# A one-core attention and FFN kernel: six of its eight norms transposed by DMA

## The reference

```
x = x + tanh(g_xattn[0]) * attention(layernorm(x), ctx, ctx, Wq, Wk, Wv, Wd)
x = x + tanh(g_ffn[0])   * (layernorm(x) @ dequantize(qweight).T + bias)

attention(q, k, v):            # x, ctx: 32 x 64 x 512;  32 heads in 8 groups, head size 128
    Q = (q @ Wq.T) as (b, s, 8, 4, 128);  K, V = (k @ Wk.T), (v @ Wv.T) as (b, s, 8, 128)
    scores = Q . K * 128**-0.5, causal;  probs = softmax(scores)
    return (probs . V as (b, s, 4096)) @ Wd.T
```

## Time and profile before

| | |
|---|---|
| median of 3 runs | 1074.34 us (1073.34 to 1075.73) |
| the profiled execution | 1073.39 us, its span 1071.6 us |
| TensorE busy | 1027.7 us, 96% |
| VectorE, ScalarE, GpSimd busy | 670.9, 474.8, 236.8 us |
| TensorE's granted clock | 0.994 of full speed |

### The profile page before, as it was taken

How to read it: one execution, slowest core, us unless ns; L and a number is a source line. 1 busy time by engine, 2 the same in 40 slices (tenths; PEclk the granted TensorE clock), 3 DMA queues, 4 the chain that set the end, 5 groups by cost and what they waited for, 6 DMA issues and landing times.

```text
span 1071.6 us, 20150 instructions
## 1 busy us (share of the span) xinstructions
PE 1027.7 (96%) x8000; PEld 577.8 (54%) x8000; DVE 670.9 (63%) x1361; ACT 474.8 (44%) x937; POOL 236.8 (22%) x245
## 2 busy tenths in 40 slices
PE   5899999999999999999999999999999999999995
PEld 3455554555555555555555555555555555555542
DVE  6856666666578566655566566555557655555688
ACT  5767676576534243353334323254433423333322
POOL 1545465465504100010003110010000300000013
PEclk9999999999999999999999999999999999999997
DMA  7757644435245133233321443312323332223211
GB/s 274 238 163 250 217 175 160 158 129 177 98 150 197 50 129 118 104 114 118 119 84 55 177 158 119 118 53 86 119 106 112 119 118 89 65 106 131 72 35 59
DMA packets 64251, 137.08 MB, mean 128 GB/s; under 512 B 5409, under 2 KB 38177, under 8 KB 53537
## 3 DMA queue, kind: packets, MB, share of 16 engines
q1 hardware_dynamic: 64160, 135.81, 36.9%
HBM read 93.85 MB, written 25.17 MB: 111 GB/s over the span
## 4 chain that ended last, share of the span: by engine, by line
PE 84%; DVE 7%; ACT 6%; issue 2%; DMA 0%; SPq 0%; POOL 0%; DVEq 0%; ACTq 0%; POOLq 0%
PE pa L1210 39%; PE py L1210 30%; PE av L1321 5%; PE pp L1304 2%; PE ps L1290 2%; PE py L1382 2%; PE pp L1290 2%; PE av L1358 1%; ACT junk L567 1%; ACT q L628 1%; ACT junk L577 1%; DVE q L833 1%; ACT wd L623 1%; DVE sc L879 1%; DVE sc L890 1%
## 5 line engine op out<-in xcount | busy, mean ns | idle before, releaser
L1210 PE MATMUL pa<-xT,wq 128*128 128x512 f16 x1536 | 342.4, 379 | 6.4 <-DVE q L833 3.5
L1210 PE MATMUL py<-wd,att 128*128 128x512 f16 x1488 | 337.1, 379 | 0.0
L1210 PEld LDWEIGHTS pa<-xT,wq 128*128 128x128 f16 x1536 | 146.0, 98 | 186.6 <-issue 18.9
L1210 PEld LDWEIGHTS py<-wd,att 128*128 128x128 f16 x1488 | 143.8, 98 | 156.2
L628 ACT ACTIVATE q<-pa 128x512 f16<-128x512 f32 x128 | 75.8, 592 | 249.4 <-PE pa L1210 249.4
L912 DVE SCALAR_TENSOR_TENSOR xacc<-py,f_y,xacc 128x512 f32<-128x512 f32 x128 | 95.9, 749 | 137.0 <-PE py L1210 136.9
L674 ACT ACTIVATE att<-av 128x256 f16<-128x256 f32 x256 | 80.8, 385 | 152.2 <-PE av L1321 151.8
L903 DVE SCALAR_TENSOR_TENSOR att<-av,att 128x256 f16<-128x256 f32 x256 | 93.4, 417 | 66.0 <-ACT att L674 66.0
L833 DVE SCALAR_TENSOR_TENSOR q<-pa,q 128x512 f16<-128x512 f32 x128 | 87.8, 686 | 66.6 <-ACT q L628 63.8
L1210 PE MATMUL pa<-wv,cT 128*128 128x128 f16 x1536 | 96.2, 219 | 0.0
L1210 PEld LDWEIGHTS pa<-wv,cT 128*128 128x128 f16 x1536 | 89.8, 98 | 0.9
(11 more groups left out here) (127 smaller groups left out, 1095.2 us busy)
## 6 DMA issues: line engine op xcount, KB each, us to landing
wq<-kept_q SPq DMA_DIRECT2D x24, 1024.0 KB, 7.0
wd<-kept_d SPq DMA_DIRECT2D x23, 1024.0 KB, 4.8
v_dup<-v_nat SPq DMA_DIRECT2D x128, 128.0 KB, 2.4
raw_d<-in_wdT SPq DMA_DIRECT2D x8, 1024.0 KB, 8.8
kept_q<-wq SPq DMA_DIRECT2D x8, 1024.0 KB, 7.4
kept_d<-wd SPq DMA_DIRECT2D x8, 1024.0 KB, 4.9
raw_q<-in_wqT SPq DMA_DIRECT2D x7, 1024.0 KB, 5.7
wk<-kept_k SPq DMA_DIRECT2D x24, 256.0 KB, 7.2
```

What stands on the lines that cost most here:

```text
L1210: last = pe.matmul(out, stationary(a, i), moving(b, i), start=(i == 0 and (a, b) == PASSES[0]), stop=(i == count - 1 and (a, b) == PASSES[ ...
```

## The change

The four-tile transposes of all norms but the first and the last leave TensorE and ScalarE. SyncE instead issues for each of those norms 32 DMAs with `transpose=True`, each from 128x128 of `xh` to 128x128 of `xT` (`transpose_norm`, behind `duplicate_v`). The readers of `xT` wait for their count on a new semaphore `xT_ld` (`transposed`). Norms of kind 2 now write `xh` with its columns in the order that the transposes of before picked them in (`permuted`). Block 1's norm moves from step 6 to step 5 with all its engines' work, and the FFN of blocks 0 and 1, with its stores, from g = 1 to g = 2.

```diff
@@ norm_step
-            return 6 if tb == 0 else 4
+            return 5 if tb == 0 else 4
@@ readers of xT
+        def transposed(eng, call):
+            if call == 0:
+                eng.wait_ge(xT_ok, TILES)
+            else:
+                eng.wait_ge(xT_ld, 16 * 2 * KC * TILES * call)
@@ ffn_of
-            if g == 1 and 0 < tb < BLOCKS - 1:
+            if g == 2 and 0 < tb < BLOCKS - 1:
@@ sync
+            def transpose_norm(call):
+                which, tb = NORMS[call]
+                if which == 1:
+                    wait(sp, q_mm, 4 * GROUPS * (tb - 1))
+                    wait(sp, f_mm, TILES * (tb - 1))
+                else:
+                    sp.wait_ge(q_mm, 4 * GROUPS * (tb + 1))
+                for t in range(TILES):
+                    sp.wait_ge(x_hi, TILES * call + t + 1)
+                    wait_x_lo(sp, TILES * call + t)
+                    for c in (HI, LO):
+                        for i in range(KC):
+                            sp.dma_start(xT[:, tb % 2, c, i, t * P:(t + 1) * P], xh[:, t, c, i * P:(i + 1) * P],
+                                         transpose=True).then_inc(xT_ld, 16)
...
                 if m < STEPS:
                     duplicate_v(m)
+                if norm_of(n) is not None:
+                    transpose_norm(norm_of(n))
@@ gpsimd and vector ln_lo, scalar ln_hi (output and inputs)
+            def permuted(part, t):
+                if NORMS[t // TILES][0] == 1:
+                    return part
+                return part.rearrange("p (j i) -> p i j", j=KC)
...
-                pool.tensor_tensor(xh[:, t % TILES, LO, :], xn[:, t % TILES, :], xh[:, t % TILES, HI, :],
-                                   ALU.subtract).then_inc(x_lo, 1)
+                pool.tensor_tensor(permuted(xh[:, t % TILES, LO, :], t), straight(xn[:, t % TILES, :], t),
+                                   permuted(xh[:, t % TILES, HI, :], t), ALU.subtract).then_inc(x_lo, 1)
@@ scalar
                     for t in range(TILES):
                         ln_hi(TILES * call + t, g == 0)
-                    for t in range(TILES):
-                        ln_out(TILES * call + t)
@@ tensor
-                        pe.wait_ge(xT_ok, TILES * (NORMS.index((1, tb)) + 1))
+                        transposed(pe, NORMS.index((1, tb)))
...
-                if j < 2 and n > 0 and norm_of(n - 1) is not None:
-                    pe.wait_ge(xT_ok, TILES * (norm_of(n - 1) + 1))
...
                 y_unit(n, 2)
-                if call is not None:
-                    ln_transpose(TILES * call, 4 * n + 4)
-                    ln_transpose(TILES * call + 1, 4 * n + 4)
                 y_unit(n, 3)
-                if call is not None:
-                    ln_transpose(TILES * call + 2, 4 * n + 4)
-                    ln_transpose(TILES * call + 3, 4 * n + 4)
```

More of the change, by code:

```diff
@@ L176, in build @@
         xT_mm, xT_ok = sem("xT_mm"), sem("xT_ok")
+        xT_ld = sem("xT_ld")
         q_mm, q_hi, q_lo = sem("q_mm"), sem("q_hi"), sem("q_lo")
@@ L255, in build @@
         LATE = tuple(range((BLOCKS - 2) * TILES, (BLOCKS - 1) * TILES))
+        FINAL = len(NORMS) - 1
+        def transposed(eng, call):
[3 more added lines that the diff above has]
+                eng.wait_ge(xT_ld, 16 * 2 * KC * TILES * call)
         def ffn_of(n):
             g, tb = n % GROUPS, n // GROUPS
-            if g == 1 and 0 < tb < BLOCKS - 1:
+            if g == 2 and 0 < tb < BLOCKS - 1:
                 return tb - 1
@@ L470, in split_wv, with straight @@
                 weight_lo(wv[:, g % 2, LO, :, :], raw_v[:, g % 2, :, :], wv[:, g % 2, HI, :, :], w_mul[:, g, 2:3], wv_lo)
+            def permuted(part, t):
+                if NORMS[t // TILES][0] == 1:
+                    return part
+                return part.rearrange("p (j i) -> p i j", j=KC)
+            def straight(part, t):
+                if NORMS[t // TILES][0] == 1:
+                    return part
+                return part.rearrange("p (i j) -> p i j", j=KC)
             def ln_lo(t):
                 pool.wait_ge(x_hi, t + 1)
-                pool.tensor_tensor(xh[:, t % TILES, LO, :], xn[:, t % TILES, :], xh[:, t % TILES, HI, :],
-                                   ALU.subtract).then_inc(x_lo, 1)
+                pool.tensor_tensor(permuted(xh[:, t % TILES, LO, :], t), straight(xn[:, t % TILES, :], t),
+                                   permuted(xh[:, t % TILES, HI, :], t), ALU.subtract).then_inc(x_lo, 1)
             def ln_rstd(call):
@@ L641, in v_part, with permuted, straight @@
                                scale=K_SCALE).then_inc(v_hi, 1)
+            def permuted(part, t):
+                if NORMS[t // TILES][0] == 1:
+                    return part
+                return part.rearrange("p (j i) -> p i j", j=KC)
+            def straight(part, t):
+                if NORMS[t // TILES][0] == 1:
+                    return part
+                return part.rearrange("p (i j) -> p i j", j=KC)
             def ln_hi(t, summed):
+                call = t // TILES
                 act.wait_ge(xn_ok, t + 1)
-                wait(act, xT_mm, t - TILES + 1)
-                at = NORMS[t // TILES][1] * TILES + t % TILES
-                act.activation(xh[:, t % TILES, HI, :], xn[:, t % TILES, :], ACT.Copy,
+                if call > 0 and t % TILES == 0:
+                    transposed(act, call - 1)
+                at = NORMS[call][1] * TILES + t % TILES
+                act.activation(permuted(xh[:, t % TILES, HI, :], t), straight(xn[:, t % TILES, :], t), ACT.Copy,
                                accum_out=x_sum[:, at:at + 1] if summed else None).then_inc(x_hi, 1)
             def ln_out(t):
-                act.wait_ge(xT_mm, t + 1)
+                done = t % TILES + (TILES if t >= TILES else 0)
+                act.wait_ge(xT_mm, done + 1)
                 par = NORMS[t // TILES][1] % 2
@@ L995, in ln_lo @@
                 dve.wait_ge(xn_ok, t + 1)
-                dve.tensor_tensor(xh[:, t % TILES, LO, :], xn[:, t % TILES, :], xh[:, t % TILES, HI, :],
-                                  ALU.subtract).then_inc(xd_lo, 1)
+                dve.tensor_tensor(permuted(xh[:, t % TILES, LO, :], t), straight(xn[:, t % TILES, :], t),
+                                  permuted(xh[:, t % TILES, HI, :], t), ALU.subtract).then_inc(xd_lo, 1)
             def ffn_weight(j):
@@ L1346, in ln_transpose @@
                 wait_x_lo(pe, t)
-                wait(pe, xT_ok, t - 1)
+                if t % TILES >= 2:
+                    pe.wait_ge(xT_ok, t % TILES - 1 + (TILES if t >= TILES else 0))
                 wait(pe, av_hi, av_before)
@@ L1352, in ln_transpose @@
                     for i in range(KC):
[L1353 to L1356, removed]
+                        part = xh[:, t % TILES, c, i * P:(i + 1) * P]
                         at = (c * KC + i) * P
@@ L1364, in ffn_unit @@
                 if t % TILES == 0 and t not in FFN_DVE:
-                    pe.wait_ge(xT_ok, TILES * (NORMS.index((2, t // TILES)) + 1))
+                    transposed(pe, NORMS.index((2, t // TILES)))
                 if t in FFN_DVE:
-                    pe.wait_ge(xT_ok, TILES * NORMS.index((2, t // TILES)) + t % TILES + 1)
+                    pe.wait_ge(xT_ok, TILES + t % TILES + 1)
                 if t == LATE[0]:
```

## The result

The changed kernel takes 1237.31 us in the median of four runs (1235.25 to 1242.85), beside 1075.03 us for the kernel before: a ratio of 1.152, with a 95% interval of 1.150 to 1.155. I had forecast 1138.4 us with a range up to 1200. The sign was right, the size was not. The profiled execution spans 1235.9 us, 164.3 us more than before.

What follows compares the result with a forecast made beforehand. The prediction took TensorE as the bound, busy 1027.7 of 1071.6 us. Added to the profiled 1073.39 us, 54.8 us for five norms and 9.3 for block 1 gave 1137.5; 0.95 for the median made 1138.4 us, range 1058 to 1200.

Steps and rivals of the forecast that it cites:

- What the change can give: Six norms' transposes off TensorE save 2.92 us each in two and 2.74 in four: 16.8 us at most.
- The room: SyncE's queue has 16.7 us for a norm's 32 DMAs before the next step's `wd` load makes TensorE wait.
- The price of a transposing DMA: Each holds SyncE's queue 0.95 us, the root of 0.38 x 2.4; 32 take 30.4 us a norm.
- the same formula: With c per DMA: 5 x (wait - 2.74) + 1.6, wait = 32c - 16.7; from c = 0.71, 32c - 22.7 more for block 1.
- (d): Rival: two transposing DMAs in flight on SyncE's queue, c = 1.2 us each, 1186 us; chance 0.26.
- The estimate of 1207 us: The same sum with the Trainium skill's 1309 ns for each DMA on SyncE's queue gives 1207 us.
- Rival (c): The forecast's own case: SyncE's queue time per DMA from 0.62 to about 1.1 us, 1078 to 1163 us; chance 0.37.
- GpSimd's lateness in step 6: Block 1's norm in step 5 delays GpSimd's `wd`, so step 6's first `y_unit` waits 4.5 us.
- The `wq` of step 8: Behind block 1's 32 DMAs and `kept_q`, `wq` lands at 281.8, making step 8's query product 7.7 us late.
- The permuted write: Writing `xh` with permuted columns in norms of kind 2 was allowed 0 to 2 us, in the last norm only.
- The FFN's move: Moving the FFN and its stores from step 1 to step 2 of a pass was costed at nothing.

Runs made afterwards that it cites:

- e11_block1_tensor: `e10_ffn_step1` with block 1's norm of step 6 transposed by TensorE again: 1063.32 us, 0.9903 of the kernel before.
- e4_strided_read: The changed kernel with the permuted `xh` written in address order and `xn` read in strides of four instead: 1224.09 us.
- e10_ffn_step1: The changed kernel with one transposing DMA a tile, address-order write with strided read, block 1's norm in step 6, FFN back at g = 1: 1066.44 us.
- e7_clock_whole_wait: The changed kernel with 98 overwritten filler products on TensorE before step 9's first `y_unit`, 121 in steps 13, 17, 21, 25: 1234.09 us.

## Why the prediction was wrong, point by point

- **What the change can give, 16.8 us.** It can't be read alone in any run. `e11_block1_tensor` keeps five of the six norms off TensorE, a saving of 13.9 us by my figures, and is 11.2 us faster, with a last norm that its strided read makes slower. The size holds roughly.
- **The room, 16.7 us.** Right at 32, 16 and 4 DMAs a norm. The queue's time less the wait is 21.5, 16.4, 15.2, 16.4 and 15.2 us in the five norms, 16.9 in the mean. In step 9, the first, there was more because TensorE itself came late, from the wait for queries. The place of the waits was right too.
- **The price of a transposing DMA, 0.95 us. This step failed.** It is 41.81 / 32 = 1.31 us. I took the middle between a plain issue and `v_dup`'s landing time on a scale of ratios, a choice no row backed. A price error of 0.36 us stands 32 times in each of six norms: with 1.31 in the same formula the sum is 5 x (25.2 - 2.74) + 1.6 + 19.2 = 133 us, 1207 us in all. Of the 99 us between forecast and result this is 69 by the formula, and 62 by the waits themselves (`wd` and `wq` 138.1 us, forecast 76.2). My reason for going above `v_dup`'s 0.61 (a finer cut on one side) has nothing for it either: a DMA of eight such blocks costs the same. Of the rivals, (d) with 1.2 us (1186 us) came nearest; its picture of two in flight is not shown by anything here. The estimate of 1207 us that stands under it was nearer still, and my range ended at 1200, below that. Rival (c) was also added up a little low: c = 1.1 gives 1167 us, not 1163.
- **The pages.** The Trainium skill, "VectorE: DVE Perf Modes", section "The three transpose paths", has 1309 ns for a 128x128 by DMA. The trace agrees (1.31 us each), and adds that it is a time in which the issuing queue is held. "Advanced Engine Details and Errata", section "X-Bar Transpose (TRN2)", says they are as fast as regular DMAs; here the queue needs 1.31 us where a plain one took 0.33 to 0.38, while the time to landing, 2.3 us, is about that of `v_dup`, 2.4.
- **Block 1.** GpSimd's lateness in step 6: predicted 4.5 us, 4.9 waited. The `wq` of step 8: with 1.31 us the formula gives 19.2 us, 15.1 waited. The landing it gives, 293.3, is near the 292.87 of the trace by luck: `wq` could be issued 4.2 us after `kept_q`, not 7.4, but then took 8.1, not 7.0, and the first DMA went out 1.7 us later than I had it. TensorE came 3.6 us later than in the sum, mostly because step 6's first `y_unit` ran at the lower clock (5.14 us in place of 2.75).
- **The permuted write, 0 to 2 us.** Undersized: 13.2 us by `e4_strided_read`. I looked for it only where no queue covers it, did not ask for its size (a factor of four), and overlooked that SyncE's first DMA waits for the first tile's slow halves, so that the queue starts later too. The Trainium skill, "SBUF — State Buffer", has a note on lines of 16 bytes (section "Door 1: The DMA port swizzle (why `[64,N]` ≈ `[32,N]`)") by which each access that crosses to a new line pays a penalty. The write agrees (2.5 to 2.9 us against 0.63 for 128x512); the strided read of float32 also steps 16 bytes each time, and there the penalty is far smaller (1.17 us at most in `e10_ffn_step1`).
- **The clock.** Missing from the sum: some 10 us, by the stretches of `e7_clock_whole_wait`. Before, TensorE hardly stopped and was granted 0.994 of full speed; a forecast of long waits should carry a term for what follows them.
- **The FFN's move, nothing.** 3.3 us in `e10_ffn_step1`, in a kernel without the long waits. In the changed kernel it was not measured.

By these estimates together 133 + 13 + 10 = 156 of 162 us. They are no exact sum, since the formula's 133 is 7 more than what the trace shows in its place (123.0 + 15.1 + 4.9 of waits less the 16.8 saved: 126.2).

The two traces can be compared term by term. TensorE waits 123.0 + 15.1 + 4.9 = 143.0 us for `wd`, `wq` and GpSimd, 8.5 us more for queries and 5.6 us more for high halves in the last norm; its two large groups are 19.5 us longer and its transposes 13.0 us shorter. That makes 163.6 of the 164.3 us between the two spans.

## What to carry to other kernels

Count instructions on a queue, not bytes: before moving work to DMAs, multiply the hold of one by the number in a row, and compare with the time from there to the reader of the next load in that queue. A price that no row shows and that is multiplied by 192 decides the forecast, so its upper end should be taken as seriously as its middle. And an edit that seems only to rearrange addresses, such as a permuted write, should be priced with the engine that does it.

## What the runs showed of the hardware

- A transposing DMA within SBUF holds SyncE's queue for 1.23 to 1.27 us in the median at 128x128, 128x256 and 128x1024 alike; it lands after 2.3 us and, at 128x1024, 3.1 us.
- ScalarE's 128x512 write of halves 256 bytes apart takes 2.5 to 2.9 us against 0.63 in order, and the read of its sum behind it 0.51 against 0.20 us. With the strides on the read side it takes 1.15 us.
- VectorE's work on other SBUF tiles slows while GpSimd works: such an operation then takes up to about as long as one of GpSimd's. In the changed kernel GpSimd needs 10.32 / 4 = 2.58 us for a half, and VectorE's 0.43 us become 2.58; with GpSimd's in-order writes before, 5.05 / 4 = 1.26 us and 1.27 (the last two rows of this section). So it is not the strided write alone that does this; the write makes it last longer. The operations that take `py` from PSUM (L966) stay at 0.73 to 0.75 us. The first row falls in a time in which only ScalarE writes so:

```profile
352.92 0.43 DVE L1075 CAST ff_w<-raw_d 128x512 f16<-128x512 int32 x1
...
356.18 2.58 DVE L1075 CAST ff_w<-raw_d 128x512 f16<-128x512 int32 x1
```

```profile
353.37 10.32 POOL L515 TENSOR_TENSOR xh<-xn,xh 128x512 f16<-128x512 f32 x4 [7.69 <-ACT xh L702]
```

Before, at the end of step 8:

```profile
330.19 1.27 DVE L1009 CAST ff_w<-raw_d 128x512 f16<-128x512 int32 x1
```

```profile
328.71 5.05 POOL L474 TENSOR_TENSOR xh<-xn,xh 128x512 f16<-128x512 f32 x4 [5.94 <-ACT xh L647]
```
